# Causal attention on one NeuronCore: one 96-row operand stack for all heads, and a vector engine loop of one unit

## The reference

```
scores = jnp.einsum('bqhd,bkhd->bhqk', Q, K) / math.sqrt(D_K)
scores = jnp.where(causal, scores, -jnp.inf)
attn = jax.nn.softmax(scores, axis=-1)
out = jnp.einsum('bhqk,bkhd->bqhd', attn, V)
```

```
num = jnp.einsum('bhtf,bhtfd->bhtd', phi_q, kv_cum)
den = jnp.einsum('bhtf,bhtf->bht', phi_q, jnp.cumsum(phi_k, axis=2))[..., None] + EPS
```

## Time and profile before

| | us |
|---|---|
| median of three runs | 2921.2 |
| the profiled execution's own time | 2923.05 |
| its span, first to last instruction | 2921.2 |
| pass a, first to last matmul | 263.6 to about 1218 |
| pass b, first to last matmul | 2047.7 to about 2657 |

### The profile page before, as it was taken

One profiled execution on the slowest core, in us unless ns is written; L12 is line 12 of the kernel. 1 busy time (PEld: TensorE's weight loads), 2 busy tenths in 40 slices (PEclk: granted clock), 3 DMA queues, 4 the chain that ended last, 5 costly groups with the idle time before them and its releaser, 6 DMA issues. The chain is left out here.

```text
span 2921.2 us, 59972 instructions
## 1 busy us (share of the span) xinstructions
PE 2497.1 (85%) x15239; PEld 1151.5 (39%) x15239; DVE 2235.0 (77%) x5893; ACT 1789.2 (61%) x2938; POOL 581.1 (20%) x652
## 2 busy tenths in 40 slices
PE   2687999999999999667999997993999999996656
PEld 1342333333333333254666664552222222223545
DVE  5887888888888888386777767996667666666968
ACT  0442666666666666515777756883777777773446
POOL 0445111121111111240000000223222222222200
PEclk9897899999999999898999998997999999998879
DMA  5496232323233232260000002555544444444403
GB/s 171 149 287 197 74 105 73 109 84 98 85 96 94 88 93 88 72 192 1 0 0 0 0 1 70 183 183 172 144 138 138 142 144 136 137 129 124 131 1 115
DMA packets 244357, 309.97 MB, mean 106 GB/s; under 512 B 40513, under 2 KB 178449, under 8 KB 244241
## 3 DMA queue, kind: packets, MB, share of 16 engines
q1 hardware_dynamic: 243792, 307.50, 34.4%
q10 hardware_dynamic: 448, 1.31, 0.2%
HBM read 181.29 MB, written 126.88 MB: 105 GB/s over the span
## 5 line engine op out<-in xcount | busy, mean ns | idle before, releaser
L905 ACT ACTIVATE a_p<-psum 128x1024 f32<-128x1024 f32 (+3 forms) x768 | 588.2, 813 | 302.6 <-PE psum L1008 298.1
L905 ACT ACTIVATE b_p<-psum 128x512 f32<-128x512 f32 (+5 forms) x768 | 453.6, 654 | 167.8 <-PE psum L1008 167.0
L960 DVE CUSTOM_DVE_ANT_0 a_dump<-psum,a_bias 128x128 bf16<-128x128 f32 (+3 forms) x1024 | 445.5, 487 | 106.8 <-PE psum L997 75.5
L1008 PE MATMUL psum<-b_qs,b_ks 96*128 96x512 bf16 (+7 forms) x1536 | 321.6, 331 | 38.0 <-DMA b_vs<-values 37.7
L958 DVE TENSOR_REDUCE a_peak<-psum 128x1 f32<-128x512 f32 x512 | 325.8, 685 | 21.2 <-PE psum L997 19.9
L1022 PE MATMUL psum<-b_p,b_vs 128*32 128x512 f32 (+3 forms) x3072 | 329.0, 500 | 8.0 <-POOL b_p L878 8.0
L997 PE MATMUL psum<-a_ks,a_qs 112*128 112x128 bf16 (+2 forms) x1008 | 295.0, 337 | 39.2 <-DVE a_peak L960 19.5
L937 DVE COPY b_twin<-psum 128x512 f32<-128x512 f32 (+3 forms) x384 | 213.3, 556 | 150.2 <-PE psum L1008 148.5
L878 POOL TENSOR_SCALAR_AFFINE_SELECT a_p<-a_p 128x512 f32<-128x512 f32 x256 | 162.8, 636 | 766.7 <-ACT a_p L905 766.7
L878 POOL TENSOR_SCALAR_AFFINE_SELECT b_p<-b_p 128x512 f32<-128x512 f32 x256 | 162.8, 636 | 458.6 <-DVE b_p L940 441.2
L1008 PE MATMUL psum<-a_qs,a_ks 114*128 114x512 bf16 x1008 | 248.2, 328 | 3.4 <-ACT a_p L905 1.8
(11 more groups left out here) (203 smaller groups left out, 3695.1 us busy)
## 6 DMA issues: line engine op xcount, KB each, us to landing
qk_parts<-l_parts SPq DMA_DIRECT2D x96, 256.0 KB, 3.1
qk_parts<-g_parts SPq DMA_DIRECT2D x96, 256.0 KB, 2.8
b_qs<-qk_parts SPq DMA_DIRECT2D x160, 128.0 KB, 2.8
b_ks<-qk_parts SPq DMA_DIRECT2D x155, 128.0 KB, 2.9
values<-l_vx SPq DMA_DIRECT2D x64, 256.0 KB, 3.3
sums<-a_osb SPq DMA_DIRECT2D x64, 256.0 KB, 2.5
m_num<-sums SPq DMA_DIRECT2D x64, 256.0 KB, 3.8
m_inv<-reciprocals SPq DMA_DIRECT2D x64, 256.0 KB, 4.5
```

What stands on the lines that cost most here:

```text
L905: act.activation(p[s % SLOTS][:, 2 * k:2 * k + heads, q0(s):512], m.psum[:, at:at + heads, q0(s):512], ACT.Exp if softmax else ACT.Square, ...
L960: last = dve.tensor_tensor_reduce(dump[c % SRING][:, at:at + w], piece, bias[:, 512 - w:], 1.0, NEG, ALU.add, ALU.max, dst)
L1008: last = pe.matmul(m.bank[score_bank(s, hd)][:, q0(s):512], ks[r][live, hd, kt * P:(kt + 1) * P], qs[r][live, hd, h * 512 + q0(s):(h + 1) ...
```

## The change

The parts are stored in DRAM in their natural order, and all four heads have the same 96 rows: the three K parts against Q high, two against Q middle, one against Q low. A unit is loaded by seven DMAs: pairs of 48, 32 and 16 rows over all four heads (8 KB in a row, where it was 4 KB), and V. There is no gap any more, so pass b needs no fixed rows, and pass a only those above the stack. The rows with the maxima move from 112 and 113 to 96 and 97, and matmuls contract 96 rows (98 with the maxima) for every head. In pass a VectorE's loop has one unit in its body and 30 iterations, followed by one unit's rest; the other engines keep loops of three units. One semaphore counts the arrival of the maxima rows in place of three.

```diff
-            sp.wait_ge(first_set, 4)
+            sp.wait_ge(first_set, 2)
...
-            sp.wait_ge(first_loaded, 16 * 15)
+            sp.wait_ge(first_loaded, 16 * 7)
...
-def set_rows(z, eng, q, k, softmax, step, done):
-    low, high = slice(32, MAIN), slice(STACK, P)
-    some, wide = slice(z.HPU // 2, z.HPU), slice(0, z.HPU if softmax else z.HPU // 2)
-    for tile, rows, heads, fill in ((q, low, some, 0.0), (q, high, wide, 0.0), (k, low, some, 0.0), (k, high, wide, 1.0)):
-        eng.memset(tile[rows, heads, :], fill).then_inc(step, 1)
-        done += 1
-        eng.wait_ge(step, done)
+def set_rows(eng, q, k, step, done):
+    eng.memset(q[STACK:P, :, :], 0.0).then_inc(step, 1)
+    eng.wait_ge(step, done + 1)
+    eng.memset(k[STACK:P, :, :], 1.0).then_inc(step, 1)
+    eng.wait_ge(step, done + 2)
...
-    half = z.S * z.HPU // 2
-    pairs = []
-    for par, runs in enumerate((((0, 1, 2, 0, 2), (32, 2, 2, 0, 2), (64, 0, 0, 1, 2)),
-                                ((64, 1, 2, 0, 2), (96, 2, 1, 1, 1), (0, 2, 1, 0, 1), (16, 0, 0, 1, 2)))):
-        heads = slice(par * half, (par + 1) * half)
...
+    pairs, row = [], 0
+    for q_part, groups in ((0, 3), (1, 2), (2, 1)):
+        into = slice(row, row + z.DK * groups)
+        q_rows = parts[0][:, q_part:q_part + 1, :]
+        pairs.append((q[into, :], q_rows.to_broadcast([z.DK, groups, width]) if groups > 1 else q_rows))
+        pairs.append((k[into, :], parts[1][:, 0:groups, :]))
+        row += z.DK * groups
...
-        LOADED = 16 * 15
+        LOADED = 16 * 7
...
-                pairs = unit_operands(z, m, qs[0], ks[0], vs[0], 0)
-                sp.wait_ge(q_set, 2)
...
-            else:
-                pool.memset(ks[0][32:MAIN, HPU // 2:HPU, :], 0.0).then_inc(k_set, 1)
-                pool.memset(ks[0][STACK:P, 0:HPU // 2, :], 1.0).then_inc(k_set, 1)
-                pool.wait_ge(k_set, 2)
...
-            if not first:
-                dve.memset(qs[0][32:MAIN, HPU // 2:HPU, :], 0.0).then_inc(q_set, 1)
-                dve.memset(qs[0][STACK:P, 0:HPU // 2, :], 0.0).then_inc(q_set, 1)
-                for r in range(1, RING):
-                    set_rows(z, dve, qs[r], ks[r], softmax, rows_set, 4 * (r - 1))
...
-            all_units(dve, unit)
+            with dve.Fori(0, UNITS - 2) as n:
+                maxima(n + 1, EARLY, CP)
+                largest(n + 1, (rows_loaded, ROWS_LOADED * n + ROWS_LOADED))
+                maxima(n + 2, 0, EARLY)
+            maxima(UNITS - 1, EARLY, CP)
+            largest(UNITS - 1, (rows_loaded, ROWS_LOADED * (UNITS - 1)))
```

More of the change, by code:

```diff
@@ L40 @@
 PARTS = 3
-Q_SLOT = (1, 2, 0)
-K_SLOT = (1, 0, 2)
 STACK = 16 * 6
-MAIN = 16 * 4
-TOP = 16 * 7
 class Sizes:
@@ L559, in _ @@
         def _(pool):
-            set_rows(z, pool, first[0], first[1], True, first_set, 0)
+            set_rows(pool, first[0], first[1], first_set, 0)
             pool.sem_inc(low_done, 2)
@@ L677, in store_parts @@
         for which in range(2):
-            slot = (Q_SLOT, K_SLOT)[which][part]
-            rows = m.qk_dram[slot, which, bass.ts(i, z.D), u * z.GT:(u + 1) * z.GT].rearrange("(c p) t -> p c t", p=P)
+            rows = m.qk_dram[part, which, bass.ts(i, z.D), u * z.GT:(u + 1) * z.GT].rearrange("(c p) t -> p c t", p=P)
             eng.dma_start(rows, parts[:, part, 2 * which:2 * which + 2, :]).then_inc(stored, 16)
-def set_rows(z, eng, q, k, softmax, step, done):
-    low, high = slice(32, MAIN), slice(STACK, P)
-    some, wide = slice(z.HPU // 2, z.HPU), slice(0, z.HPU if softmax else z.HPU // 2)
-    for tile, rows, heads, fill in ((q, low, some, 0.0), (q, high, wide, 0.0), (k, low, some, 0.0), (k, high, wide, 1.0)):
-        eng.memset(tile[rows, heads, :], fill).then_inc(step, 1)
-        done += 1
-        eng.wait_ge(step, done)
+def set_rows(eng, q, k, step, done):
[3 more added lines that the diff above has]
+    eng.wait_ge(step, done + 2)
 def unit_operands(z, m, q_tile, k_tile, v_tile, n):
+    width = z.HPU * z.S
     q, k = [tile[:, :, :].rearrange("p h t -> p (h t)") for tile in (q_tile, k_tile)]
@@ L774, in attend_pass @@
             rows, = sb("rows", [P, 2, HPU * ST], BF16)
-            rows_loaded = sm(*[f"rows_loaded{r}" for r in range(RING)])
             (bias_zero, bias_ready, peak_set, s_ready, s_taken, npeak_ready, high_ready, split_ready,
-             rows_ready) = sm("bias_zero", "bias_ready", "peak_set", "s_ready", "s_taken", "npeak_ready",
-                              "high_ready", "split_ready", "rows_ready")
+             rows_ready, rows_loaded, rows_set) = sm("bias_zero", "bias_ready", "peak_set", "s_ready", "s_taken",
+                                                     "npeak_ready", "high_ready", "split_ready", "rows_ready",
+                                                     "rows_loaded", "rows_set")
             ROWS_LOADED = 16 * 8
@@ L782, in attend_pass @@
             twin_ready, d_ready = sm("twin_ready", "d_ready")
-        rows_set, q_set, k_set = sm("rows_set", "q_set", "k_set")
         block = ctx.enter_context(nc.Block())
[L786 to L790, removed]
+        OPERAND = slice(0, STACK + 2 if softmax else STACK)
         def q0(s):
@@ L813, in load @@
             def load(n, r):
-                if not isinstance(n, int) or n >= RING:
-                    sp.wait_ge(rows_set, 4 * (RING - 1))
-                else:
-                    sp.wait_ge(rows_set, 4 * n)
+                if softmax:
+                    sp.wait_ge(rows_set, 2 * n if isinstance(n, int) and n < RING else 2 * (RING - 1))
                 pairs = unit_operands(z, m, qs[r], ks[r], vs[r], n)
@@ L824, in load_rows @@
                 for k in range(2):
-                    at = qs[r][TOP + k:TOP + k + 1, :, :].rearrange("o h (q b i) -> o (h q) b i", b=4, i=32)
+                    at = qs[r][STACK + k:STACK + k + 1, :, :].rearrange("o h (q b i) -> o (h q) b i", b=4, i=32)
                     for b in range(4):
-                        sp.dma_start(at[:, :, b, :], rows[32 * b:32 * b + 32, k, :]).then_inc(rows_loaded[r], 16)
+                        sp.dma_start(at[:, :, b, :], rows[32 * b:32 * b + 32, k, :]).then_inc(rows_loaded, 16)
             def store(n, h):
@@ L975, in largest @@
                               ).then_inc(rows_ready, 1)
[L977 to L982, removed]
             maxima(0, 0, CP)
@@ L996, in maximum_scores @@
                     for qt, h, at, w in pieces:
-                        last = pe.matmul(m.bank[SB + c % SRING][:, at:at + w], qs[r][0:TOP, hd, qt * P:(qt + 1) * P],
-                                         ks[r][0:TOP, hd, h * 512:h * 512 + w], start=True, stop=True)
+                        last = pe.matmul(m.bank[SB + c % SRING][:, at:at + w], qs[r][0:STACK, hd, qt * P:(qt + 1) * P],
+                                         ks[r][0:STACK, hd, h * 512:h * 512 + w], start=True, stop=True)
                     last.then_inc(s_ready, 1)
@@ L1006, in scores @@
                 for hd in (2 * k, 2 * k + 1):
-                    live = operand_rows(hd)
-                    last = pe.matmul(m.bank[score_bank(s, hd)][:, q0(s):512], ks[r][live, hd, kt * P:(kt + 1) * P],
-                                     qs[r][live, hd, h * 512 + q0(s):(h + 1) * 512], start=True, stop=True)
+                    last = pe.matmul(m.bank[score_bank(s, hd)][:, q0(s):512], ks[r][OPERAND, hd, kt * P:(kt + 1) * P],
+                                     qs[r][OPERAND, hd, h * 512 + q0(s):(h + 1) * 512], start=True, stop=True)
                 last.then_inc(st_ready, 1)
```

13 lines of the change are left out of this document (2 added, 11 removed).

## The result

The changed kernel takes 2898.73 us in the median of 20 runs, the kernel before 2918.65 in 20 runs of the same comparison. The ratio is 0.9933, with a 95% interval of 0.9917 to 0.9949: 15 to 24 us are won, where 76 had been forecast. The two spans differ by 32.6 us, and 10 of them lie where nothing was changed: from the end of pass a to the end of the features pass (806.8 us for 815.3) and behind pass b (262.8 for 264.6).

The account below looks back on a forecast made before the run. TensorE bounds pass b; pass a loses time to late V and VectorE's branch gaps. Terms -43.3 - 26.9 + 2 - 1.6 - 2 - 4.5 = -76.3 from 2923.05 give 2846.8, forecast 2845 us for the median; range 2836 to 2905.

Parts of the forecast that it names:

- Loads in pass a: Pass a, SyncE's loads: 7 DMAs in place of 15 land V before TensorE asks, so its wait goes: -43.3 us.
- VectorE's loop: Pass a: the one-unit loop loses the gaps at the branch back, -26.9 us, with +2 added for 29 branches.
- Rival 2: Pass a loads: transfer at 168 GB/s or less leaves V as late as now; -9.1 us in all, 2912; chance 0.08.
- Rival 3: Pass a: the clean unit of 26.52 us is not reached; 0.5 us more per unit, +15, 2860; chance 0.05.
- Start of pass a: Unit 1's load: fewer fills and issues move it earlier and remove TensorE's wait of 1.63 us: -1.6 us.
- Latent pass: ScalarE's 4.22 us wait for stores shrinks with eight issues less on SyncE's queue: -2 us (0 to -4.2).
- Start of pass b: Unit 0's loads, without fills and from two queues, let the first matmul start earlier: -4.5 us (-2.1 to -5.7).
- The matmuls: TensorE's matmuls: contracting 96 rows instead of 112 or 114 changes nothing: 0 us.

Follow-up runs that it names:

- the loop alone: The kernel before, with only VectorE's loop in pass a changed to the changed kernel's loop of one unit: ratio 1.0004 against the kernel before.
- the reversed stack: The changed kernel with 48-row DMAs at rows 48 to 95, 32-row at 16 to 47, 16-row at 0 to 15: ratio 0.9780, median 2853.73 us.
- the hold: The changed kernel, SyncE holding unit 1's load at pass b's start until unit 0's landed: single run, 13.25 us to the first matmul in place of 19.87.

## Why the prediction was wrong, step by step

**Loads in pass a: forecast -43.3, measured +2.5.** This is the step that failed, and 45.8 of the 56 us by which the sum missed. The chain of the argument was right up to its last link: SyncE starts as before, seven issues end after 4.1 us, the transfer bounds then, and TensorE asks after 12.35 us. The last link was "At 229 GB/s 2.1 MB take 9.2 us". That rate was measured on DMAs of 16 and 32 rows on both halves of the partitions, and used for DMAs of 48 rows at 0 to 47. (In the kernel before, heads 2 and 3 have their blocks in the rows 0 to 47 and 64 to 111, with the gap at 48 to 63, as the numbers in `unit_operands` give them, and not in 0 to 31 and 48 to 111.) With the new DMAs it was 186 GB/s in the window of pass a (over the whole load, 2.1 MB in 13.2 less 1.6 us, an estimate is 181) and 157 at the start of pass b, and V landed 13.2 us after the start in place of 10.8; before it had been 13.9 (9.7 for the issues and 4.2 for V). The 1.6 us to arrive are not at fault: in the kernel before the first packets come about 1.4 us (load at 711.02) to 1.8 us (2033.41) after the issue. A slack of 1.5 us had been drawn from a rate that no row showed for these rows of SBUF. The forecast took 168 GB/s for "plainly an issue rate" (0.58 busy). That may hold for the old DMAs, and it said nothing of the new ones. With other rows the same seven DMAs bring V in time, and the whole -43 appears: the term's size was right for a layout that the change did not have.

**VectorE's loop: forecast -26.9, +2, measured -26.9 and 0.** All second halves are clean, and 29 branches cost nothing that the marks can show. That fits a body short enough to be held, as argued; between 124 and 368 rows nothing was tried. The way against the change that the rule of the Trainium skill (Runtime: NRT & Kernel Launch, "Instruction fetch mechanics") leaves open, a block replaced before the branch, was not seen in any of the 29. But the term was no gain by itself: with V late, the loop alone gave all of it back.

**Rival 2, given 0.08, is what happened**: the load is bound by transfer. Its rate of 168 GB/s or less was too low for pass a (181 to 186), so V came 0.7 us earlier and not as late as before. Its sum of -9.1 charged the nine units the full 2.2 us each, +19.5. The loop alone shows 67.3 in these 29 units for the old load, 24.0 over 43.3; V landing 0.7 us earlier in each of them, 20.3, takes that to about the 45.8 seen. Its gains at the start of the two passes did not come. That 2898.73 lies within the stated 2836 to 2905 is owed to that range alone, which was drawn out part of the way to rival 2; the forecast's own ended at 2858. Rival 3 did not happen: the clean unit is still 18.05 + 8.47.

**Start of pass a: forecast -1.6, measured 0.** The wait for V at 287.81 went, and TensorE then stood for VectorE's maxima instead:

```profile
288.17 1.91 PE L966 MATMUL psum<-a_ks,a_qs 96*128 96x512 bf16 x5 [1.06 <-DVE a_peak L931]
```

From the first matmul to the first copy of the sums it is 50.5 us, 50.2 before.

**Latent pass: forecast -2, measured about +1.** ScalarE's wait grew from 4.22 us to 5.17, since the DMA engines and not SyncE's queue were short, and the new DMAs hold them longer: from 144 to 152 us they are busy 1.00 at 158 GB/s, before 0.75 at 199. With the reversed stack the wait is 4.0.

```profile
161.54 2.06 ACT L595 ACTIVATE l_parts<-psum 128x512 bf16<-128x512 f32 x4 [5.17 <-DMA qk_parts<-l_parts]
```

**Start of pass b: forecast -4.5, measured +3.4** (19.9 for 16.4). It was the rate again, and more than the 0.4 MB of unit 1's load that was taken to compete: the 6.6 us that the hold gave back are 1.1 MB at 160 GB/s.

**The matmuls: forecast 0, measured 0.** In pass b 710 scores of 96 rows took 382 ns on average, had 384 and 379; those of 98 rows in pass a took 379 and 381 (for the tiles `a_` and `first_`). Pass b lasted 608.2 us against 608.9.

The sum of what was measured (loads, branch, start of pass a, latent pass, start of pass b, length of pass b) is 2.5 - 26.9 + 0.3 + 1 + 3.4 - 0.7 = -20.4, against 19.9 between the medians.

## What to carry to other kernels

Before a sum relies on a transfer being in time, compare the rows of SBUF on which the new DMAs fall with those of the rate that is used; here the same bytes in the same seven DMAs landed at 13.2, 12.0 or 11.5 us, with only their rows changed. When two losses never fall on the same unit, one may be hiding the other: each of the two edits was worth nothing alone, and both with the 48 rows at 32 to 79 were worth 70 us. And where a load is late, ask first whether part of it could start earlier; splitting off V, which alone needed the late slot, was worth as much as any layout (0.9754 against 0.9762).

## What was not expected of the hardware

A DMA of 384 KB on rows 0 to 47 landed 5.3 us after its issue, on rows 32 to 79 or 48 to 95 after 4.1, with the DMA engines shown as busy in either case: a share near 1.0 doesn't tell that the engines move what they can (0.99 at 186 GB/s here, 0.98 at 229 in the earlier trace rows). Cutting its rows from 8 to 4 KB changed the landing of the whole load by nothing (13.2 us), and reading one DRAM row three times over cost nothing (5.3 us for Q's 48 rows, 5.2 with three different rows).
